# Norm and quantisation of the last feed-forward's input, moved tile by tile into the last head pair of layer-1 attention

## The reference, cut to what matters

```
x = x + attn1(layernorm(x))            # block-sparse attention, 16 heads of 64, window of 3 blocks of 64, 2 global blocks
x = x + ffn1(layernorm(x))

ffn1(h): hq = round(h * 127/max|h|) / (127/max|h|)       # per token
         g  = hq @ ternary(w1).T                         # 1024 -> 4096
         g  = silu(depthwise conv over 3 tokens(g) + b)
         y  = quantised(g) @ ternary(w2).T               # 4096 -> 1024
```

## Time and profile before

| | us |
|---|---|
| median of 3 runs | 2360.39 (2360.01 to 2364.5) |
| the profiled execution's own time | 2361.38 |
| its span, core 4, the slowest | 2359.9 |
| spans of the 8 cores | 2347.9 to 2359.9 |
| PE busy in the span | 1980.6 (84%) |
| DVE busy | 1165.7 (49%) |
| ACT busy | 1095.4 (46%) |
| POOL busy | 28.8 (1%) |

### The profile page before, as it was taken

The page is one execution under the profiler, slowest core; times in us unless marked ns, Lnnn a source line. Parts: engine busy times, 40 slices in busy tenths (PEclk is TensorE's granted clock), DMA queues, the critical chain, the costliest instruction groups (busy, mean ns, idle before and its releaser), DMA issues. The chain is left out here.

```text
span 2359.9 us, 34886 instructions; the slowest of 8 cores (2347.9 to 2359.9 us)
## 1 busy us (share of the span) xinstructions
PE 1980.6 (84%) x12314; PEld 921.0 (39%) x12314; DVE 1165.7 (49%) x2056; ACT 1095.4 (46%) x1986; POOL 28.8 (1%) x72
## 2 busy tenths in 40 slices
PE   3688887888879999599998888877795499979999
PEld 2433333332334444244444444443442244434444
DVE  3222444433444542241463666666655688876442
ACT  3465555565431110011222777776743778874221
POOL 0000000000000000000000000000000000000000
PEclk9799878877889999799999899888797599989999
DMA  8001333440018850664001000000202122223332
GB/s 213 2 1 37 108 125 126 143 99 1 1 42 218 231 169 1 134 178 70 3 1 25 13 11 11 10 11 2 37 2 73 72 63 79 74 85 112 107 107 89
DMA packets 60071, 170.09 MB, mean 72 GB/s; under 512 B 3840, under 2 KB 36608, under 8 KB 48896
## 3 DMA queue, kind: packets, MB, share of 16 engines
q1 hardware_dynamic: 53536, 134.31, 16.9%
q0 software_dynamic: 6368, 33.56, 8.7%
HBM read 167.85 MB, written 33.55 MB: 85 GB/s over the span
## 5 line engine op out<-in xcount | busy, mean ns | idle before, releaser
L653 PE MATMUL f0R<-lnT,wgu 128*128 128x512 bf16 x1536 | 337.4, 383 | 27.9 <-DMA wgu<-f0wgu_d 27.9
L419 ACT ACTIVATE a0bq<-a0S 128x1024 bf16<-128x1024 f32 (+1 forms) x320 | 266.5, 894 | 191.2 <-PE a0S L344 190.6
L653 PEld LDWEIGHTS f0R<-lnT,wgu 128*128 128x128 bf16 x1536 | 151.7, 99 | 213.3 <-issue 35.7
L688 ACT ACTIVATE f0si<-f0R 128x1024 bf16<-128x1024 f32 x48 | 49.1, 1023 | 389.2 <-PE f0R L653 389.2
L1287 PE MATMUL g1hp<-g1q1T,g1t 128*128 128x512 bf16 x1024 | 225.0, 381 | 5.5 <-DVE g1a L1407 4.2
L1311 PE MATMUL g1hp<-g1t,g1q1T 128*128 128x512 fp8e4 x1024 | 222.9, 381 | 1.8 <-ACT g1q1T L1362 1.8
L361 PE MATMUL a0y<-a0bq,a0vv 128*64 128x512 bf16 (+3 forms) x640 | 131.5, 406 | 50.9 <-ACT a0bq L419 20.2
L714 DVE TENSOR_TENSOR f0hT<-f0si,f0R 128x1024 bf16<-128x1024 bf16 x48 | 58.6, 1222 | 227.9 <-PE f0R L653 227.9
L1084 ACT ACTIVATE a1pt<-a1T 128x768 bf16<-128x768 bf16 (+2 forms) x152 | 118.5, 785 | 113.0 <-PE a1T L969 102.8
L1287 PEld LDWEIGHTS g1hp<-g1q1T,g1t 128*128 128x128 fp8e4 x1024 | 98.4, 98 | 131.9 <-issue 19.2
L1311 PEld LDWEIGHTS g1hp<-g1t,g1q1T 128*128 128x128 bf16 x1024 | 100.5, 98 | 123.9 <-issue 4.2
(11 more groups left out here) (189 smaller groups left out, 2934.6 us busy)
## 6 DMA issues: line engine op xcount, KB each, us to landing
a0wst<-g1w_d SPq DMA_DIRECT2D x32, 1024.0 KB, 4.8
f0wst<-g1w_d SPq DMA_DIRECT2D x32, 1024.0 KB, 6.0
hs_scr<-g1hsp SPq DMA_DIRECT2D x32, 512.0 KB, 3.2
g1q1T<-hs_scr SPq DMA_DIRECT2D x8, 2048.0 KB, 10.5
wgu<-f0wgu_d POOLq DMA_DIRECT2D x24, 512.0 KB, 6.9
xs<-x SPq DMA_DIRECT2D x4, 2048.0 KB, 26.0
t_scr<-f0wt SPq DMA_DIRECT2D x32, 256.0 KB, 2.5
g1t<-t_scr SPq DMA_DIRECT2D x2, 4096.0 KB, 15.1
```

The costliest lines, as they stand in the source:

```text
L419: s.activation(bq[:, u % 4, :, n0:512], sS[:, u % 2, :, n0:512], AF.Square).then_inc(s_sq, 1)
L653: mm = t.matmul(R[:, k % 4, 512 * n2:512 * (n2 + 1)], wgu[:, cc % 3, x, j, :], lnT[:, j, t0 + 512 * n2:t0 + 512 * (n2 + 1)], start=(j == 0 ...
```

## The change

Norm and quantisation leave the prologue of the last feed-forward and enter `a1_order`. The helper `finish(k)` stands where the two W halves of a tile stood, and also lists N (statistics on DVE, 1/sqrt on ACT, the normed float32 tile `lx` on POOL), Z (for the tile before: largest magnitude, reciprocal and the rounded product on DVE, and the bf16 tile `q1c` on POOL) and Q (for two tiles before: 8 transposes on PE into a `pj` bank, copied by ACT into `q1T`). To make room on DVE, the four products of X move to POOL for the last pair alone, and V's take-out moves to ACT. N uses `norm_dve_stats`, `norm_act_rstd`, `norm_pe_transpose` and `norm_act_evac`, which stood in the kernel and serve the layers before; the `Ln` helpers of the prologue go. The ternary `t1` is stored chunk by chunk ([chunk, j, 128]); its first 12 chunks are loaded by SP in the middle of attention into memory that the first half's values no longer need, and the other 20 at the start of the feed-forward, where PE waits for them at chunk 12. `t2` now has memory of its own and is loaded at once.

```diff
 def a1_order():
+    done = list(range(1, NT)) + [0]
+    def finish(k):
+        if k >= 1:
+            out.append(("Z", k - 1, done[k - 1]))
+        out.extend([("W", done[k], 0), ("W", done[k], 1)])
+        if k >= 2:
+            out.append(("Q", k - 2, done[k - 2]))
+        out.append(("N", k, done[k]))
...
         elif i < len(items) and m >= 5:
-            out += [("W", m - 4, 0), ("W", m - 4, 1)]
-    out += [("W", ti, n2) for ti in (13, 14, 15, 0) for n2 in range(2)]
-    return out
+            finish(m - 5)
+    for k in range(12, NT):
+        finish(k)
+    return out + [("Q", 14, done[14]), ("Z", 15, done[15]), ("Q", 15, done[15])]
...
 # GpSimd, behind its weight loads
+                    if it[0] == "X" and it[1] == 7:
+                        m = it[2]
+                        g.wait_ge(s_rr, m + 1)
+                        if m < 16:
+                            for u in range(1 if m == 0 else 0, 2):
+                                lo = 64 if u == 0 else 0
+                                g.tensor_scalar(pp[:, m % 2, u, lo:lo + 192], pp[:, m % 2, u, lo:lo + 192],
+                                                rr[:, m % 2, 0, u:u + 1], None, ALU.mult)
+                                x = g.tensor_scalar(pp[:, m % 2, u, 256:384], pp[:, m % 2, u, 256:384],
+                                                    rr[:, m % 2, 1, u:u + 1], None, ALU.mult)
+                        else:
+                            x = g.tensor_scalar(pr_[:, :], pr_[:, :], rr[:, 2, 0, 0:1], None, ALU.mult)
+                        x.then_inc(s_p7, 1)
+                    elif it[0] == "N":
+                        g.wait_ge(N.rs, k + 1)
+                        g.tensor_scalar(lx[k % 2][:, :], xs[:, ti, :], N.mv[:, ti, 0:1], N.rstd[:, ti:ti + 1],
+                                        ALU.subtract, ALU.mult).then_inc(s_xh, 1)
+                    elif it[0] == "Z":
+                        g.wait_ge(s_qz, k + 1)
+                        if k >= 2:
+                            g.wait_ge(N.tp, k - 1)
+                        g.tensor_scalar(q1c[:, k % 2, :], lx[k % 2].bitcast(I32)[:, :], am[:, ti:ti + 1],
+                                        1.0 / 127.0, ALU.mult, ALU.mult).then_inc(N.ap, 1)
 # SyncE, in attention
+                sp.wait_ge(s_av, use(4, 0))
+                sp.dma_start(t1[:, 0:12, :, :], t_d[0, :, 0:12288]...).then_inc(l_t1[0], 16)
 # TensorE
+                    elif it[0] == "Q":
+                        pj_out(t, n - 2)
+                        norm_pe_transpose(t, N, q1c, ident, as_tiles(pj[:, n % 2, :]), k)
 # ScalarE
+                    elif it[0] == "V" and it[1] == 7:
+                        s.activation(yT[:, pr, 128 * m + c0:128 * (m + 1)], tb[:, b % 2, 384 + c0:512],
+                                     AF.Identity, bias=bia[:, 3, pr:pr + 1]).then_inc(s_y7, 1)
+                    elif it[0] == "N":
+                        norm_act_rstd(s, N, k, ti, 1)
+                    elif it[0] == "Q":
+                        norm_act_evac(s, N, q1T, as_tiles(pj[:, banked[it] % 2, :]), k, ti)
 # VectorE
+                    elif it[0] == "X" and it[1] == 7:
+                        v.reciprocal(rr[:, m % 2, :, u0:2], den[:, m % 2, :, u0:2]).then_inc(s_rr, 1)
+                    elif it[0] == "N":
+                        v.drain()
+                        norm_dve_stats(v, N, xs, k, ti)
+                    elif it[0] == "Z":
+                        v.wait_ge(s_xh, k + 1)
+                        v.tensor_reduce(am[:, ti:ti + 1], lx[k % 2][:, :], AX.X, ALU.max,
+                                        apply_absolute_value=True)
+                        v.drain()
+                        v.tensor_scalar(am[:, ti:ti + 1], am[:, ti:ti + 1], 1e-5, None, ALU.max)
+                        v.drain()
+                        v.reciprocal(ra[:, ti:ti + 1], am[:, ti:ti + 1])
+                        v.drain()
+                        v.tensor_scalar(lx[k % 2].bitcast(I32)[:, :], lx[k % 2][:, :], ra[:, ti:ti + 1], 127.0,
+                                        ALU.mult, ALU.mult).then_inc(s_qz, 1)
 def emit_l1ffn
-                sp.dma_start(t1[:, :, :], t_d[0, :, :]...).then_inc(l_t1, 16)
-                sp.wait_ge(L.ap, NT)
+                sp.dma_start(t1[:, 12:32, :, :], t_d[0, :, 12288:]...).then_inc(l_t1[1], 16)
                 sp.dma_start(t2[:, :, :], ...)
-                for ti in range(NT):
-                    ln_pe_transpose(t, L, q1c, ident, tps, ti)
-                t.wait_ge(L.ev, NT)
-                t.wait_ge(l_t1, 16)
                 for c in range(NC):
+                    if c in (0, 12):
+                        t.wait_ge(l_t1[c // 12], 16)
```

More of the change, by code:

```diff
@@ L799, in emit_l1attn @@
     for it in order:
-        if it[0] in ("P", "W") or it[0] == "A" and it[2] == 0:
+        if it[0] in "PWQ" or it[0] == "A" and it[2] == 0:
             banked[it] = len(banked)
@@ L806, in emit_l1attn @@
     users = [it for _, it in users]
-    on_act = [it[0] == "P" and it[1] == "q" for it in users]
-    freed = [(a, sum(x == a for x in on_act[:n + 1])) for n, a in enumerate(on_act)]
+    by = ["n" if it[0] == "Q" else "q" if it[:2] == ("P", "q") else "p" for it in users]
+    freed = [(x, by[:n + 1].count(x)) for n, x in enumerate(by)]
     n_pre = 24
@@ L842, in emit_l1attn @@
         pr_ = place(nc, p + "pr", 136, [128, T], BF16)
+        lx = [place(nc, p + f"lx{i}", 120 - 8 * i, [128, D], F32) for i in range(2)]
+        q1c = place(nc, p + "q1c", 12, [128, 2, D], BF16)
+        am = sb("am", [128, NT], F32)
+        ra = sb("ra", [128, NT], F32)
         bo = sb("bor", [1, D], BF16)
@@ L869, in _ @@
                 g.memset(one[:, :], 1.0)
+                g.memset(N.rstd[:, NT:NT + 1], LN_EPS)
                 g.memset(pp[:, :, 0, 0:64], 0.0)
@@ L959, in _ @@
                         b = use(pr, m, k)
-                        t.wait_ge(s_p, item(pr, m) + 1)
+                        if pr == 7:
+                            t.wait_ge(s_p7, m + 1)
+                        else:
+                            t.wait_ge(s_p, item(pr, m) + 1)
                         if b >= 2:
@@ L1126, in _ @@
                                         negate=True).then_inc(s_mx, 1)
+                    elif it[0] == "X" and it[1] == 7:
+                        _, pr, m = it
+                        v.wait_ge(s_x, item(pr, m) + 1)
+                        if 2 <= m < 16:
+                            v.wait_ge(s_p7, m - 1)
+                        if m < 16:
+                            u0 = 1 if m == 0 else 0
+                            v.reciprocal(rr[:, m % 2, :, u0:2], den[:, m % 2, :, u0:2]).then_inc(s_rr, 1)
+                        else:
+                            v.reciprocal(rr[:, 2, 0, 0:1], den[:, 2, 0, 0:1]).then_inc(s_rr, 1)
                     elif it[0] == "X":
@@ L1487, in build_fused @@
                    wqk, a1wqk, w_qk, wv, a1wv, w_v)
-        emit_l1attn(nc, "a1", xs, lnT, ident, wqk, a1wqk, w_qk, wv, a1wv, w_v, a1wo, a1bias, a1bo)
-        emit_l1ffn(nc, "g1", xs, ident, tsc, t_d, g1cw, g1cb, hs_d, x_out)
+        l_t1 = [es.enter_context(nc.semaphore(f"l_t1{i}")) for i in range(2)]
+        q1T = place(nc, "q1T", 48, [128, ND, T], BF16)
+        t1 = place(nc, "t1", 0, [128, 32, ND, 128], F8)
+        emit_l1attn(nc, "a1", xs, lnT, ident, wqk, a1wqk, w_qk, wv, a1wv, w_v, a1wo, a1bias, a1bo,
+                    q1T, t1, t_d, l_t1)
+        emit_l1ffn(nc, "g1", xs, ident, tsc, q1T, t1, l_t1, t_d, g1cw, g1cb, hs_d, x_out)
     return nc
```

146 lines of the change are left out of this document (38 added, 108 removed).

## The result

The changed kernel is slower: 1.0112 times the kernel before, 95% interval 1.0092 to 1.0131, with 2387.3 to 2388.6 us where the kernel before had 2360.0 to 2364.5. The forecast was 2343, faster.

A forecast was written before the change was run, and what follows sets the result against it. PE bounds the last pair before; afterwards a ring through POOL at 7.8 us a tile. Removing the 72 us prologue, with 54 paid back, puts the feed-forward 18.2 us earlier: 2361.4 becomes 2343, whole range 2335 to 2364.

The forecast's parts named there:

- POOL's price: GpSimd's time for 1024 elements in the last attention pair: 1.3 us plus 0.1 handover, bounds 0.9 and 2.3.
- Rival 2: GpSimd is slow: over 19 units of 1024 elements the gain is gone at 2.25 us each; 2371 at 2.8; chance 0.14.
- first W to the end of the first statistics: Start of the last pair's W-carrying steps, with 1.5 us for earlier steps and 1.28 for ln's table load: 10.3 us.
- 11 rings and the row's maximum: Last pair's W-carrying steps: 85.8 us for 11 rings, plus 1.2 for the row item's maximum over 2048 elements.
- the row item: Between the rings and the last tiles: POOL's product of 2048 elements, transposes, copies, A, then W and statistics; 16.5 us.
- three last rings: The last tiles of attention after the row item, at 7.8 us each: 23.4 us.
- tail: From the last statistics to the first feed-forward matmul, all in series, with q1c, transposes and copy: 8.6 us.
- stretch: From the first W to the first feed-forward matmul, the part the change rewrites: forecast 145.8 us.
- the table load for ln: ACT was to load the table for ln at the first tile's statistics in the last pair: 1.28 us.
- the forecast's ring: Chain from one tile's statistics to the next in the last pair: 6.43 us plus 1.4 for POOL, 7.8 a tile.
- 1, the lower clock: PE becomes the last pair's bound at a lower clock: 2354 mild, chance 0.12; 2382 if low throughout, 0.04.
- 3, DVE and POOL in each other's way: DVE's double-rate product waits for POOL's small product in progress, at most 0.35 a ring: 5.6 us, 2349; chance 0.10.

The follow-up runs named there:

- The probe: Kernel before, with fourteen forms of GpSimd's tensor_scalar and a copy added at its idle start; subtract and multiply with two per-partition scalars took 3.78 us.
- The fast forms: Changed kernel, with GpSimd's normed tile as multiply and add behind a one-column product nb, X's products with a second multiply by 1.0; 0.9967 times the kernel before.
- Z behind N: Z of the tile before listed behind W and N: in the changed kernel 1.0028 times the kernel before, on top of the fast forms 0.9880 (step of 8.63).
- the late load: Changed kernel, with the first 12 chunks of the first weights loaded at the feed-forward's start, not during attention; 1.0166 times the kernel before.

## Why the prediction was wrong

**The step that failed is POOL's price**, "I take the middle of the first two, 1.3": it measured 3.78 for the normed tile, outside even the bounds of 0.9 to 2.3. I priced a unit of 1024 elements from a memset and a select, instructions of another kind, and took all of POOL's products as one unit. The probe shows that there is no such unit: of the three, q1c (multiply, multiply) is at 1.12, near the forecast 1.3, the row product (a multiply alone) at 5.44 for 2.4, the normed tile (subtract, multiply) at 3.78. The range rested on those bounds, so it fell with them. Rival 2 had the right place and the right sign, at 0.14; its break-even of 2.25 us a unit was passed by two of the three.

**The rest of the sum holds in total, by misses that cancel.** With everything measured from the first W on core 1, against the forecast:

| term | forecast | measured | of it by POOL's prices |
|---|---|---|---|
| first W to the end of the first statistics | 10.3 | 7.8 | |
| 11 rings and the row's maximum | 87.0 | 111.5 | 11 x 2.5 = 27 |
| the row item | 16.5 | 24.1 | 2.5 + 3.0 |
| three last rings | 23.4 | 30.3 | 3 x 2.5 = 7 |
| tail | 8.6 | 11.3 | 2.5 |
| stretch | 145.8 | 184.9 | 42 |

42 us of price on 145.8 would give 188, 3 more than measured. The first term is 2.5 short. 1.3 of that is the table load for ln, which does not occur: ACT loads a table five times in the changed kernel's trace and six times before, and between 1246.3 and 1910.3 not once, although N's ln and exp run there. The rest is W's first two halves, 2.79 and 1.90 us for the 3.59 and 2.14 of core 4 before. The rings are 2.5 below forecast and price, since their other links take 7.6 for 7.8 and the row's maximum adds 0.35 for 1.2. The row item is 2.1 longer than forecast and price give. The fast forms are the test of the forecast's ring at nearly its own price: a normed tile of 1.19 with 0.4 for nb, a step of 7.94 for 7.8 and a stretch of 149.5 for 145.8. Their whole time, 0.9967, did not come down to the forecast 2343 all the same; in the profiled execution the slowest core's later first W is most of what is missing.

**Rivals.** 1, the lower clock: PEclk was 0.83 in the steps (windows above), near the rival's own mean of 0.81, yet a step stays at 10.1, since PE has 2.7 us to spare. It cost nothing there. With shorter rings it does cost: 0.2 us in each of the fast forms' steps at 0.81 to 0.83, and 1.8 in the one step of 8.63 with Z behind N. (The prediction's terms of a step at 1.2 GHz add up to 11.0, not 10.8, which changes nothing here.) 3, DVE and POOL in each other's way: it exists, but off the ring. In the timeline above the small product beside DVE's takes 1.05 us where its like takes 0.60, and DVE's keeps its 0.75, also against the small product that was still in progress when it started, for which the rival had it wait; with Z behind N it is DVE's that loses. The Trainium skill (SBUF — State Buffer, section "Who interferes with whom") says that the later of the two waits until the other ends. The rows agree with that only in part: the small product started at 1750.53, DVE's ended at 1751.12, and 0.60 after that would be 1751.72, but it ended at 1751.58. And with Z behind N, DVE's product ended at 1817.65, inside POOL's slow tile that began first and ran to 1819.70: there it did not wait for the end. The measurement decides.

**Outside the stretch** the forecast holds. The first W comes at 1710.3 in the median of cores 0 to 3, at 1708.0 over the eight cores before; the forecast had 1.5 for that. From the first feed-forward matmul to the end of the span it is 483.2 us in the median, before and after. Inside this, the first weights' matmuls take longer, from 1900.8 to 2132.1 on core 1, 231.3 for 228.7 before. Half of that is one wait of PE for DVE at the third chunk, 1.63 for 0.35. The difference is as long as ACT's table load (1.28), which now stands ahead of the first chunk's instruction on ACT and stood behind the second's before. The other half, and what makes both good later, was not taken apart.

The forecast said of the load of t1 that it is hidden before and after; the late load shows that this is the early load's doing, by 8.5 us.

## What to carry to other kernels

Where the sum rests on an instruction whose kind is nowhere in the trace, the bounds have to come from the same kind of instruction or be left wide; a probe of a dozen forms at the idle start of a kernel settles it in one run. When work moves between engines inside a loop, write down the ring from an operation to itself one tile later: each link in it costs its full length, and listing the waiting part one step later takes it out, provided that what else the queue carries is not late in turn. An engine that is given work "to make room" elsewhere should be checked for whether the room was needed; here VectorE waited for GpSimd 3.5 us a step and had it anyway.

## What the runs showed of the hardware that was not expected

On GpSimd, `tensor_scalar` over 128x1024 takes 1.12 us for multiply and multiply, 1.19 for multiply and add, 2.85 for a single multiply and 3.6 to 3.8 for subtract and multiply. Two columns as scalars, a column and a constant, or two constants made 0.16 us of difference in the last of these, and bf16 for float32 as its output none. Over 192 elements of bf16 a single multiply takes 0.77 and the pair 0.43. Multiply and multiply from float32 to int32 took 1.12 too (the rounded product on GpSimd). VectorE's double-rate product of 0.753 us takes 1.34 in the median beside GpSimd's 1.19 us tile and 0.90 to 1.16 inside its 3.78 us tile. It keeps its 0.753 beside GpSimd's small products, one in progress when it starts and one that starts later and takes 1.05 for 0.60.
